# Graph attention layers: edges sorted once into 128x128 buckets and looked up by one-hot products, in place of indirect gathers in every layer

## What is computed

```python
def _transformer_conv(x, src, dst, edge_attr, Wq, bq, Wk, bk, Wv, bv, We, Ws, bs):
    q = x @ Wq + bq; k = x @ Wk + bk; v = x @ Wv + bv; e = edge_attr @ We
    alpha = jnp.sum(q[dst] * (k[src] + e), axis=-1) / jnp.sqrt(jnp.float32(D))
    amax = jax.ops.segment_max(alpha, dst, num_segments=N)
    p = jnp.exp(alpha - amax[dst])
    w = p / jax.ops.segment_sum(p, dst, num_segments=N)[dst]
    msg = (v[src] + e) * w[:, None]
    return jax.ops.segment_sum(msg, dst, num_segments=N) + x @ Ws + bs

for i in range(3):
    x = jax.nn.relu(_transformer_conv(x, ...))
    if i < 2:
        x = _layer_norm(x, ln_gamma[i], ln_beta[i])
out = _layernorm(x0 + jax.nn.log_softmax(x, axis=1))
```

## Time and profile before

| what | value |
|---|---|
| median of the runs, no profiler | 6419.34 us |
| span of the profiled execution | 10221.2 us |
| chunk steps | 372 |
| per chunk, of the median | 17.26 us |
| per chunk, of the profiled span | 27.5 us |
| PE / PE weight loads / DVE / ACT / POOL busy in the profile | 4680.2 / 3119.1 / 4304.9 / 2615.5 / 4568.1 us |
| HBM traffic of the profiled execution | 38 GB/s over the span |

### The profile page before, as it was taken

The page is one execution under the profiler, slowest core; times in us unless marked ns, Lnnn a source line. Parts: engine busy times, 40 slices in busy tenths (PEclk is TensorE's granted clock), DMA queues, the critical chain, the costliest instruction groups (busy, mean ns, idle before and its releaser), DMA issues.

```text
span 10221.2 us, 104558 instructions
## 1 busy us (share of the span) xinstructions
PE 4680.2 (46%) x25782; PEld 3119.1 (31%) x25782; DVE 4304.9 (42%) x19388; ACT 2615.5 (26%) x6114; POOL 4568.1 (45%) x4842
## 2 busy tenths in 40 slices
PE   4444444444444444444444444434444444444444
PEld 3332333333333223332333333322222323232233
DVE  3444444444444344444444444434444444444444
ACT  2222222222222222222222222222222222222222
POOL 4444444444444444444444444444444444444443
PEclk8666666666666666666666666665666565666656
DMA  3111111111111111111111111111111111111111
GB/s 83 36 39 36 39 37 39 37 39 37 37 38 36 35 37 39 37 39 37 39 37 39 37 39 37 38 34 35 37 36 35 35 38 35 35 38 36 35 37 29
DMA packets 906731, 387.54 MB, mean 38 GB/s; under 512 B 758448, under 2 KB 828848, under 8 KB 906544
## 3 DMA queue, kind: packets, MB, share of 16 engines
q1 hardware_dynamic: 751920, 228.08, 9.8%
q0 software_dynamic: 154752, 158.78, 8.1%
HBM read 362.94 MB, written 26.89 MB: 38 GB/s over the span
## 4 chain that ended last, share of the span: by engine, by line
another core or an unknown queue 51%; ACT 18%; DVE 15%; issue 10%; PE 6%; DVEq 0%; DMA 0%; ACTq 0%; SPq 0%
DVE cmax L725 6%; ACT mT L479 5%; ACT mT L481 5%; DVE score L722 3%; ACT prob L505 2%; PE agg_ps L1028 2%; DVE dot_out L715 2%; PE max_ps L988 1%; PE agg_ps L1002 1%; ACT u_mid L493 1%; ACT u_parts L492 1%; ACT lnv L514 1%; PE max_ps L992 1%; DVE score L729 1%
## 5 line engine op out<-in xcount | busy, mean ns | idle before, releaser
L442 POOL DMA_INDIRECT feat<-x_table,idx x3224 | 3041.5, 943 | 3762.5 <-DVE state L804 2744.0
L998 PE MATMUL agg_ps<-feat,prob 128*64 128x129 f32 x9672 | 2145.4, 328 | 2474.4 <-issue 2454.1
L442 POOL DMA_INDIRECT feat<-x,idx x1612 | 1526.0, 947 | 1835.7 <-DVE state L804 1372.8
L998 PEld LDWEIGHTS agg_ps<-feat,prob 128*64 128x64 f32 x9672 | 1340.9, 162 | 3068.3 <-issue 3058.2
L700 DVE TENSOR_TENSOR u_rest<-u_win,u_parts 128x129 f32<-128x129 f32 x372 | 110.0, 296 | 4581.4 <-ACT u_parts L487 2721.2
L487 ACT CAST u_parts<-u_win 128x129 bf16<-128x129 f32 x372 | 112.7, 303 | 4639.4 <-remote 4503.6
L715 DVE CUSTOM_DVE_ANT_0 dot_out<-feat,u_ps 128x129 bf16<-128x129 f32 x4836 | 1044.7, 285 | 84.3 <-issue 80.7
L981 PE MATMUL u_ps<-u_parts,mT 128*128 128x129 bf16 x4836 | 1069.7, 312 | 19.8 <-ACT mT L481 19.8
L982 PE MATMUL u_ps<-u_parts,mT 128*128 128x129 bf16 x4836 | 1076.8, 314 | 0.0
L988 PE MATMUL max_ps<-ident,cmax 128*64 128x128 f32 x372 | 145.3, 391 | 1520.4 <-DVE cmax L725 1520.4
L479 ACT ACTIVATE mT<-u_ps 64x896 bf16<-64x896 bf16 x744 | 675.7, 908 | 550.5 <-remote 542.4
(11 more groups left out here) (108 smaller groups left out, 5092.1 us busy)
## 6 DMA issues: line engine op xcount, KB each, us to landing
feat<-edge SPq DMA_DIRECT2D x372, 416.0 KB
feat<-x_table,idx POOLq DMA_INDIRECT x3224
u_win<-u_table SPq DMA_DIRECT2D x744, 48.2 KB
feat<-x,idx POOLq DMA_INDIRECT x1612
u_table<-u_out SPq DMA_DIRECT2D x248, 48.2 KB
u_table<-big SPq DMA_DIRECT2D x13, 386.0 KB
x_table<-xnew SPq DMA_DIRECT2D x248, 16.0 KB
x_table<-x SPq DMA_DIRECT2D x2, 1664.0 KB
```

The source lines that it names most:

```text
L442: nc.gpsimd.indirect_dma_start(feat[s][:, t, 0:D], None, table, bass.IndirectOffsetOnAxis(idx[s][:, t:t + 1], 0),).then_inc(rows_loaded[s] ...
L998: ins = nc.tensor.matmul(agg, prob[:, t, :], feat[s][:, t, 0:UC], start=(t == 0), stop=(t == T - 1))
```

## The change

Nodes are cut into NB = 49 blocks of 128. An edge belongs to the bucket (block of `dst`, block of `src`). Every bucket has 128 slots, the 49 diagonal ones (which also hold the self loops) 256, so a target block has NT = 50 tiles of 128 slots, 6400 slots for about 4200 edges. The fullest bucket of the reference's inputs holds 114 edges off the diagonal and 246 on it, so all fit and the general path, which the change keeps, isn't taken.

Four stages follow each other; each begins when the one ahead has ended:

1. **Fill.** ACT issues 49 DMAs that write the edge table `e_table` in HBM with empty rows, 49 x 128 x 50 rows of 272 bytes (85.3 MB). POOL waits for all of them.
2. **Sort.** For each of the 124 chunks DVE computes the slot of each edge (`key_hits`, `places`: one-hot of the 98 possible buckets, counts, ranks; PE adds up over partitions in `prefix`), and POOL scatters the rows (attributes, local `dst`, local `src`) with 13 indirect DMAs, 1612 in all.
3. **Ids.** For each block SP loads its bucket rows (1.74 MB), PE transposes the two id columns, ACT copies them and SP stores them to `id_table`.
4. **Layers.** Three layers of 49 block steps (and two more steps to empty the pipeline). The node table `x` lies in SBUF as three bf16 parts that add up to fp32 (`xp`). In step i a block is gathered (`gather`, `scores`, `maxima`), the block before it gets its exponentials and sums (soft), and the one before that its node part.

A step handles its 50 tiles in G = 10 groups of TG = 5. Its loads are `rT` and `dT`, the ids spread over all partitions (1.64 MB each), and the block's edge rows (1.74 MB).

```diff
-                for t in range(T):
-                    nc.gpsimd.indirect_dma_start(
-                        feat[s][:, t, 0:D], None, table, bass.IndirectOffsetOnAxis(idx[s][:, t:t + 1], 0),
-                    ).then_inc(rows_loaded[s] if t < T_FIRST else rest_loaded[s], 16)
+            pool.wait_ge(table_filled, 16 * NB)
+                for t in range(T):
+                    nc.gpsimd.indirect_dma_start(
+                        e_table, bass.IndirectOffsetOnAxis(slot_i[s][:, t:t + 1], 0), rowb[s][:, t, :], None,
+                    ).then_inc(scattered[s], 16)
...
+                    for t in range(q * QT, (q + 1) * QT):
+                        ins = nc.gpsimd.tensor_scalar(nm[b][:, t, :], iota_b[:], feat[b][:, 1, t, H:H + 1], 1.0, ALU.is_equal, ALU.subtract)
+                    nc.gpsimd.tensor_scalar(m, m, BIG, None, ALU.mult).then_inc(nm_ready[q], 1)
...
+                nc.vector.tensor_tensor(oh[k][:], kc, iota_k[:].unsqueeze(1).to_broadcast([P, T, KEYS]),
+                                        ALU.is_equal).then_inc(dve_step, 1)
+                nc.vector.tensor_reduce(csum[k][:], oh[k][:].rearrange("p t k -> p k t"), AX.X, ALU.add).then_inc(csum_ready, 1)
...
+                nc.vector.tensor_tensor(picked[:], oh[k][:], kcnt[:].unsqueeze(1).to_broadcast([P, T, KEYS]),
+                                        ALU.mult).then_inc(dve_step, 1)
...
+                nc.vector.tensor_scalar(rT[b][:], rT[b][:], row_id[:], None, ALU.is_equal)
+                nc.vector.tensor_scalar(dT[b][:], dT[b][:], row_id[:], None, ALU.is_equal).then_inc(oh_ready, 1)
...
+                    for part in range(3):
+                        ins = nc.tensor.matmul(x_slot(g, j), rT[b][:, t, :], xj, start=(part == 0), stop=(part == 2))
...
+                    for part in range(3):
+                        ins = nc.tensor.matmul(u_slot(g, j), dT[b][:, t, :], up[b][:, part, :], start=(part == 0), stop=(part == 2))
...
+                act.wait_ge(x_mm[g], n1)
+                nc.scalar.copy(feat[b][:, 0, g * TG:(g + 1) * TG, 0:D],
+                               x_ps[:, g % 2, 0:TG * D].rearrange("p (t d) -> p t d", d=D)).then_inc(x_sb[g], 1)
...
+                    dve.wait_ge(dve_step, before_last[t % 2])
+                    nc.vector.scalar_tensor_tensor(cmax[t % 2][:], nm[b][:, t, :], alpha[b][:, t:t + 1], cmax[t % 2][:],
+                                                   ALU.add, ALU.max).then_inc(dve_step, 1)
...
+                    ins = nc.tensor.matmul(me_ps[:, t, :], dT[b][:, t, :], m3[:], start=True, stop=True)
...
+                    ins = nc.scalar.activation(prob[k % RING][:, j, :], nm[b][:, t, :], ACT.Exp, bias=ash[:, t:t + 1])
...
+                    ins = nc.tensor.matmul(agg_sum.rearrange("p (h f) -> p h f", h=2), prob[k % RING][:, j, :], feat_of(b, t),
+                                           start=(t == 0), stop=(t == NT - 1))
```

More of the change, by code:

```diff
@@ new lines, in rows, with wait, steps, written @@
+        def rows(table, row, n):
+            return table[bass.ds(row, n), :]
+        def wait(eng, s, count):
+            if not isinstance(count, int) or count > 0:
+                eng.wait_ge(s, count)
+        def steps(eng, l, step):
+            def written(i, gather, soft, nodes, more):
+                n = l * NB + i
+                step(l, i, i % 2, n, n - 1, n + 1, gather, soft, nodes, more)
+            for i in range(4):
+                written(i, True, i >= 1, i >= 2, True)
+            with eng.Fori(0, (NB - 5) // 2) as g:
+                for k in range(2):
+                    i = eng.snap(g * 2 + (4 + k))
+                    n = eng.snap(g * 2 + (l * NB + 4 + k))
+                    step(l, i, k, n, eng.snap(n - 1), eng.snap(n + 1), True, True, True, True)
+            written(NB - 1, True, True, True, False)
+            written(NB, False, True, True, False)
+            written(NB + 1, False, False, True, False)
@@ L396, in store_u0 @@
[L396 to L406 removed]
+                sp.dma_start(rowb[s][:, :, 0:D], e).then_inc(edge_loaded[s], 16)
@@ L433, in _ @@
+            with sp.If(general):
+                general_path()
+            with sp.Else():
+                bucket_path()
         @block.gpsimd
@@ L461, in _ @@
+            pool.wait_ge(flag_ready, 1)
+            general = pool.value_load(flag_i[:], min_val=0, max_val=1)
+            with pool.If(general):
+                general_path()
+            with pool.Else():
+                for l in range(L):
+                    steps(pool, l, ahead_step)
         @block.scalar
@@ L743, in node_out @@
[L743 to L750 removed]
+            for s in range(SLOTS):
+                dve.wait_ge(scattered[s], 16 * T * GROUPS)
@@ new lines, in prefix @@
+            def prefix(k, c, n1):
+                pe.wait_ge(csum_ready, n1)
+                if c is not None:
+                    pe.sem_inc(mark, 1)
+                    pe.wait_ge(cnt_ready, c - 1)
+                nc.tensor.matmul(x_ps[:, k, 0:KEYS], before[:], csum[k][:], start=True, stop=True)
+                nc.tensor.matmul(x_ps[:, k, P:P + KEYS], ones[:], csum[k][:], start=True, stop=True).then_inc(prefix_done, 1)
+            pe.wait_ge(const_ready, 3)
+            for c in range(2):
+                prefix(c, None, c + 1)
```

2008 lines of the change are left out of this document (1220 added, 788 removed).

## The result

The changed kernel takes 11,819.95 us (median of four runs, 11,818.53 to 11,822.02), the kernel before 6419.85 us (6418.46 to 6421.15) beside it. The ratio is 1.8414, with an interval of 1.8388 to 1.8440: 84% slower. The prediction said 9800 us, 8200 to 11,700: the sign was right, the size was not, and the time lies outside the range, 1% above its upper end.

What follows compares the result with a forecast made beforehand. It took POOL's issue of indirect DMAs to bound the kernel before; for the changed kernel, start 15 + fill 300 + sort 2250 + ids 310 + layers 6940 = 9815, so 9800 us, range 8200 to 11,700.

Steps and rivals of the forecast that it cites:

- The bound: Kernel before: POOL's 4836 indirect DMAs, 1.25 us apart, make 6045 us, 94% of the median.
- the recording of PE: Kernel before: recording PE's instructions stretches waits, explaining a profiled span 1.59 times the median.
- the expected span of 26 ms: Changed kernel's profiled span: 900 PE records a step, 0.2 us each, may make it 26 ms or more.
- Sort: Sort stage: 1612 scatters x 1.25 = 2015 us of POOL plus 235 us of DVE meetings; 2250 us, bounds 2010 and 2400.
- Fill and ids: Fill and ids stages: 85.3 MB each at 283 GB/s; 300 and 310 us, bounds 265 to 360 each.
- Layers: Three layers of 49 block steps at 46 us plus 60 us a layer: 6940 us.
- POOL: a mask over 128 is like the IOTA at 0.224 us: POOL's masks in a layer step: 50 x 0.224 + 5 x 1.37 + 1.5 = 19.5 us, twice that as upper bound.
- order of waits: Layer step: no engine alone reaches 46 us; waits between PE, DVE and ACT sum to 45.5, taken as 46.
- A: Layer step: POOL's masks and DVE's maxima exclude each other; 58 us a step, 11,600 us in all; chance 0.14.
- B: Layers: PE's clock stays at 1.2 GHz; 66 us a step with the boundary, 12,760 us in all; chance 0.07.
- C: Layer step: overlap better than followed; 30 to 38 us a step, 7,500 to 8,600 us in all; chance 0.09.
- D: Layer step: faster side, DVE alone bounds it at 24 us; 6250 us in all; chance 0.05.

Runs made afterwards that it cites:

- experiment 5: Both kernels rerun with no edit: the kernel before took 6423 us (eight runs, one traced), the changed kernel 11,826 us.
- experiment 1: Changed kernel without L740, POOL's multiplication behind every ten masks: 9286.5 us, 43.1 us a step.
- experiment 2: Changed kernel with one mask in ten written and no L740, the other masks set to zero once: 9099 us.
- experiment 4: Changed kernel with all 50 masks of a step made by DVE, none on POOL, computing the same: 9688 us.
- experiment 11: Changed kernel with POOL's masks over 64 of 128 columns, the other half set to zero once, L740 unchanged: 10,359 us.
- experiment 3: Changed kernel with DVE's two one-hots made over one tile of 50, ids stored as zeros: 11,391 us.
- experiment 7: Kernel of experiment 4 with ACT's exponentials spread over later groups instead of four groups ahead: 9429 us; on one chip 9680 without and 9424 with it.
- experiment 9: Kernel of experiment 7 with three of five mask groups back on POOL, DVE making the first two ahead of its dot products: 9848 us.
- experiment 12: Last two mask groups moved to POOL, on an all-DVE-mask kernel with thirty masks early and shifted scores first (9487 us): 9812 us.

## Why the prediction came out wrong

- **The kernel before.** The bound, the pitch of 1.25 us and its 94% of the median were right for the kernel at 6420 us (experiment 5, 72% + 22% of the chain). The reason given for the span of 1.59 times the median, the recording of PE, was wrong: with 2.6 times the records the changed kernel's span is its time, and the kernel before takes 10,220 us in every run of some batches. The sum did not rest on it, but the expected span of 26 ms did.
- **Sort.** 2250 us forecast, 2267 measured. The meetings with DVE were taken as 235 us; L670's mean of 1100 ns against a median of 958 gives 1612 x 0.142 = 229. Three meetings a chunk and 0.63 us for each were not checked apart.
- **Fill and ids.** 300 and 310 forecast, 237 and 266 measured: 385 and 331 GB/s, more than the 283 that was the best row, and more than its bound at full share, 322.
- **Layers: the step that failed** is the line "POOL: a mask over 128 is like the IOTA at 0.224 us". In its place the trace has 50 x 0.71 + 5 x 3.45 = 52.8 us, with the splits of `u` and the copy (2.5), some 0.29 us around each L740 (1.4) and the stop by the one-hots (3.0) the 60 us of the step, where the sum had 19.5 and, as an upper bound, twice that. Experiments 1, 2, 4 and 11 take masks off POOL or shorten them, and each time the step gets shorter. The IOTA of that row reads no tensor and makes no comparison with a scalar of each partition. The earlier trace rows had no POOL instruction that reads a tensor, and doubling the nearest row was not a bound. The chain was built on POOL being under every other engine, so this one price put the whole order of waits behind POOL: 147 x 14.3 = 2100 us, against 2020 that were missing in all (the other stages and the layers' ends gave some back).
- **A term put at nothing.** The prediction gave no time to meetings of POOL with DVE instructions of a single input, since beside L677 an issue took 0.94 us. The one-hots have a single input and cost POOL 3.0 us a step (experiment 3). The trace of before already held a doubtful case, though a first issue may be long for another reason; L646 has a single input too:

```profile
9.74 3.17 POOL L442 DMA_INDIRECT feat<-x,idx  x1 [8.51 <-DVE idx L644]
9.85 0.99 DVE L646 TENSOR_SCALAR src_l<-src_l 128x1612 int32<-128x1612 int32 x1
```

- **The order of waits under it.** Experiment 2 shows it at 41.8 us instead of 45.5: ACT's exponentials ahead of the copy of group 3 are there, DVE's wait for them too, though 3.33 us and not 8, and experiment 7 gets 1.7 us of it back. Mis-sized were the exponentials (a duration was taken for a pitch: they are recorded with 0.39 us, as forecast, and start 0.30 apart) and the one-hots. For these the prediction took the row's 0.52 ns per element. The trace has 1.97 us for 6400 elements, 0.31 ns each, and 3.9 us for the pair. The Trainium skill, "VectorE: DVE Perf Modes", section "The perf-mode tier table", gives a tensor_scalar with bf16 data in SBUF four times the base rate, from which the prediction estimated about 3.6 us for the pair, and by that rule the trace agrees. With 3.6 the order's step would have been 42.1 us, beside the 41.8 of experiment 2; the forecast of the whole would have moved to 9300, further from 11,820, as the error lay elsewhere.
- **The rivals.** A came within 2% of the time (11,600) by luck, with the wrong mechanism: it had POOL at 36 us and DVE's maxima end to end with it. In the changed kernel POOL and DVE meet little (L1284 at a mean of 363 ns, against 347 in experiment 4 where POOL makes no masks), and POOL fills the step by itself. What it said of exclusion is real, though, in both directions (experiments 3 and 11). B is out: the granted clock in a layer is 0.77, and PE works 35 of 60 us. C is out as well: with hardly any mask made the step is 41.8 us, not 38. D needed 23 to 26.

## What to carry over

Price each operation that moves to another engine from a row of that engine and that kind of operation; where there is none, doubling the nearest row is no bound (here the mask cost 3.2 times the row), above all if that engine already bounds the kernel. When thousands of gathers are replaced by computed masks and products, count the mask, compare and copy instructions per edge as carefully as the gathers: here the masks on POOL cost 147 x 52.8 = 7760 us, more than the 4836 x 1.25 = 6045 of all indirect DMAs of before. Before work is put into a gap, add up what already runs in it and ask when its inputs arrive. And before work goes to an idle engine, ask which instructions of the busy one it will stop: in experiments 9 and 12 DVE got less to do and still became slower.

## What the runs showed of the hardware

- POOL's tensor_scalar with two operations and a scalar per partition in bf16: 503 ns over 64 and 710 ns over 128 columns; with one operation over 1280, 3452 ns (experiment 11 and the changed kernel). DVE starts the same mask, multiplication included, every 0.17 us (experiment 4).
- Two DVE one-hots over 6400 bf16 elements back to back (3.9 us), one input each, stop a POOL mask for 3.0 us (experiment 3). A POOL instruction of 3.45 us makes a DVE instruction with two SBUF inputs 2.7 us longer (experiment 11), and five DVE masks with one tensor input 3.0 us longer (experiment 12).
- The kernel before, unchanged, runs at 6420 or 10,220 us from one batch of runs to another, with the same median of 944 ns for an indirect DMA; the kernel of experiment 4 differs by less than 0.1% between two such batches (9688 and 9680 us), and the others were not run in both.
- DVE's first instruction after the turn of its loop comes late, with nothing to wait for in the trace: 63 times, 190.6 us in all, in the changed kernel, 3.0 us each, hidden there behind POOL; its cause is open:

```profile
DVE cm L1298 <- issue: 190.6, 63, 3.5
```
